# Graph attention on one core: picked keys enter VectorE's addition from PSUM with their factor moved into the exponential

## What is computed

```python
Q, K, V = ((nodes @ w + b).reshape(n, 8, 16) for w, b in (q, k, v))
row, col = edge_index                       # edges are sorted by col in the input; row groups the sums here
scores = (Q[row] * K[col]).sum(-1) / 4 + (Q[row] * (edge_attr @ we + be).reshape(-1, 8, 16)).sum(-1) / 4
es = exp(scores)                            # no maximum is taken off
w = es / (segment_sum(es, row)[row] + 1e-8)
out = segment_sum(w[..., None] * V[col], row).reshape(n, 128) @ wo + bo
```

## Time and profile before

| | |
|---|---|
| median of three runs | 4229.77 us |
| profiled execution, its own time | 4231.56 us |
| span of the profile | 4229.8 us |
| mean granted clock of TensorE | 0.958 |
| attention loop, 101 quads | 2407 to 4150 us |

### The profile page before, as it was taken

How to read it: one execution, slowest core, us unless ns; L and a number is a source line. 1 busy time by engine, 2 the same in 40 slices (tenths; PEclk the granted TensorE clock), 3 DMA queues, 4 the chain that set the end, 5 groups by cost and what they waited for, 6 DMA issues and landing times.

```text
span 4229.8 us, 87319 instructions
## 1 busy us (share of the span) xinstructions
PE 3654.2 (86%) x23947; PEld 2567.9 (61%) x23948; DVE 2605.3 (62%) x5758; ACT 1613.4 (38%) x4192; POOL 2980.4 (70%) x2979
## 2 busy tenths in 40 slices
PE   5557777259999999999997799999999999999993
PEld 3234444134454544544544488888888888888883
DVE  8999999131131221311313588888888888888887
ACT  0046666130010100100101466666666666666661
POOL 3148788777777777777777477777777777777770
PEclk8979999679999999999998899999999999999997
DMA  9635465469999999899997366666666666666661
GB/s 371 236 106 197 184 223 186 143 227 356 340 312 357 314 333 357 296 358 330 329 357 237 119 177 178 179 178 179 177 177 177 180 179 178 176 179 178 179 179 46
DMA packets 496864, 969.13 MB, mean 229 GB/s; under 512 B 279879, under 2 KB 297235, under 8 KB 494888
## 3 DMA queue, kind: packets, MB, share of 16 engines
q1 hardware_dynamic: 346872, 630.29, 44.8%
q0 software_dynamic: 118768, 243.12, 19.3%
q10 hardware_dynamic: 31168, 95.09, 6.8%
HBM read 767.81 MB, written 200.41 MB: 229 GB/s over the span
## 4 chain that ended last, share of the span: by engine, by line
PE 44%; POOL 31%; issue 13%; DVE 3%; DMA 2%; ACT 1%; DVEq 0%; POOLq 0%; ACTq 0%; SPq 0%
POOL records L1037 26%; PE ps L1158 12%; PE ps L1816 7%; PE ps L1834 7%; PE ps L1820 6%; POOL kv L1755 5%; PE ps L1809 3%; PE ps L1826 2%; PE ps L1789 2%; PE ps L1787 2%; PE ps L1444 1%; DMA records<-recs,pos 1%; PE ps L1136 1%; DMA kv<-kv_table,rec 1%; PE ps L1798 1%
## 5 line engine op out<-in xcount | busy, mean ns | idle before, releaser
L1037 POOL DMA_INDIRECT records<-recs,pos x1562 | 1586.7, 1016 | 480.7 <-issue 470.3
L1755 POOL DMA_INDIRECT kv<-kv_table,rec x1314 | 1311.2, 998 | 481.3 <-issue 440.7
L1158 PE MATMUL ps<-adj,mh 128*128 128x500 f16 (+1 forms) x6370 | 1308.3, 366 | 7.0 <-DVE mh L1309 6.1
L1158 PEld LDWEIGHTS ps<-adj,mh 128*128 128x128 f16 x6370 | 619.4, 97 | 674.8 <-DVE mh L1309 6.3
L1330 DVE TENSOR_TENSOR adj<-adj,quarter 128x128 f16<-128x128 f16 (+25 forms) x305 | 45.8, 209 | 764.7 <-DMA adj<-adj_full 756.8
L1820 PE MATMUL ps<-we,at 128*128 128x256 f32 x1616 | 466.3, 381 | 0.0
L1196 ACT ACTIVATE sc<-sc 128x1 f32<-128x1 f32 x6 | 1.2, 203 | 1216.1 <-DVE sc L1278 973.1
L1834 PE MATMUL ps<-msg,ohf 128*128 128x136 f32 x3232 | 449.0, 282 | 7.8 <-DVE msg L2006 7.8
L1816 PE MATMUL ps<-qn,oht 128*128 x3232 | 446.1, 281 | 4.2 <-ACT at L1883 1.2
L1816 PEld LDWEIGHTS ps<-qn,oht 128*128 128x128 f32 x3232 | 392.7, 192 | 47.4 <-issue 46.7
L1834 PEld LDWEIGHTS ps<-msg,ohf 128*128 128x128 f32 x3232 | 404.9, 191 | 8.9 <-DVE h L2024 8.8
(11 more groups left out here) (328 smaller groups left out, 5075.0 us busy)
## 6 DMA issues: line engine op xcount, KB each, us to landing
adj<-adj_full SPq DMA_DIRECT2D x420, 875.0 KB, 6.2
x1t<-kv_table SPq DMA_DIRECT2D x303, 256.0 KB
adj_full<-blk SPq DMA_DIRECT2D x12, 6125.0 KB, 19.0
records<-deg ACTq DMA_DIRECT2D x1, 56576.0 KB, 170.4
rec<-records SPq DMA_DIRECT2D x404, 136.0 KB
records<-recs,pos POOLq DMA_INDIRECT x1562
recs<-in_edge_attr ACTq DMA_DIRECT2D x18, 1344.0 KB, 13.3
kv<-kv_table,rec POOLq DMA_INDIRECT x1314
```

The costliest lines, as they stand in the source:

```text
L1037: G.indirect_dma_start(out=k.rec_d, out_offset=bass.IndirectOffsetOnAxis(ap=k.pos[:, at:at + 1], axis=0), in_=k.recs[:, q, j, :], in_offse ...
L1158: last = mm(bank, mh[:, part, hi, :], adj[:, c, x * width:(x + 1) * width], start=(hi == 0 and part == 0), stop=True, skip_group_check=True)
L1755: G.indirect_dma_start(out=kv[:, q, j, :], out_offset=None, in_=k.kv_d, in_offset=bass.IndirectOffsetOnAxis(ap=rec[:, q, j, RD:RD + 1].bit ...
```

## The change

The key lift goes from ScalarE's list. VectorE's addition takes all four tiles in every group; in a picked group the first tile of `kv` holds zero in its key half, written once before the loop, since no gather writes that slot, and so key and edge feature come from PSUM alone. What `goodcol` did for the keys is done in the exponential: for the first tile of a picked group the scale is a new column `goodscale` = 1/4 x `goodcol` (a marked group then gets exp(0) = 1, which its zeroed one-hot takes out of the sums). So the exponential of a picked group becomes two activations, one over tiles 1 to 3 and one over tile 0. `lifted` counts the values alone.

```diff
-            act.sem_inc(lifted, 2 * NPICK)
+            act.sem_inc(lifted, NPICK)
...
-            def lift_keys(g, q, i):
-                if q not in PICKS:
-                    return
-                done(act, "queried", g)
-                before(act, "scored", g, S)
-                act.sem_inc(sem("rec_gated"), 1)
-                A.activation(kq[:, q % S, 0, :], PS[:, 4 + q % S, 0:D], ACT.Identity, scale=goodcol[:, bass.ds(g, 1)]).then_inc(lifted, 1)
...
-                A.activation(msg[:, q, :, D:MW], sc[:, q % S, :].rearrange("p (j h) -> p j h", h=HEADS), ACT.Exp,
-                             scale=DK ** -0.5).then_inc(S_["weighed"], 1)
-            steps(act, ENG.Activation, ((lift_keys, 2), (pack, 0), (evacuate, 1), (weigh, 2), (lift_values, 2)))
+                j = GT - gathered(q)
+                scores = sc[:, q % S, :].rearrange("p (j h) -> p j h", h=HEADS)
+                last = A.activation(msg[:, q, j:GT, D:MW], scores[:, j:GT, :], ACT.Exp, scale=DK ** -0.5)
+                if j:
+                    last = A.activation(msg[:, q, 0, D:MW], scores[:, 0, :], ACT.Exp, scale=goodscale[:, bass.ds(g, 1)])
+                last.then_inc(S_["weighed"], 1)
+            steps(act, ENG.Activation, ((pack, 0), (evacuate, 1), (weigh, 2), (lift_values, 2)))
...
+            for q in PICKS:
+                V.memset(kv[:, q, 0, 0:D], 0.0)
             v.wait_ge(ends_spread, 1)
+            V.tensor_scalar(goodscale, PS[:, 1, 0:NG], DK ** -0.5, None, ALU.mult)
...
-                j = GT - gathered(q)
-                if j:
-                    v.wait_ge(lifted, i * (2 * NPICK) + (2 * (PICKS.index(q) + NPICK) + 1))
-                ch.link(V.tensor_tensor(kq[:, q % S, j:GT, :], kv[:, q, j:GT, 0:D], PS[:, 4 + q % S, j * P:].rearrange("p (j c) -> p j c", c=D), ALU.add))
+                ch.link(V.tensor_tensor(kq[:, q % S, :, :], kv[:, q, :, 0:D], PS[:, 4 + q % S, :].rearrange("p (j c) -> p j c", c=D), ALU.add))
```

More of the change, by code:

```diff
@@ L1603, in attend @@
         basecol = of(k.x1t, NG).bitcast(I32)
-        goodcol, badcol = of(k.x1t, NG), of(k.x1t, NG)
+        goodcol, badcol, goodscale = of(k.x1t, NG), of(k.x1t, NG), of(k.x1t, NG)
         given[0] = 0
@@ L1621, in attend @@
         wl = [sem(f"rows_loaded{q}") for q in range(len(PICKS))]
-        spotted, picked, lifted = sem("spots_turned"), sem("values_picked"), sem("keys_and_values_lifted")
+        spotted, picked, lifted = sem("spots_turned"), sem("values_picked"), sem("picked_values_lifted")
         NPICK, NONE = len(PICKS), 65536.0
@@ L2011, in message @@
                 if q in PICKS:
-                    v.wait_ge(lifted, i * (2 * NPICK) + (2 * (PICKS.index(q) + NPICK) + 2))
+                    v.wait_ge(lifted, i * NPICK + (PICKS.index(q) + 1 + NPICK))
                 weighted(q, slice(0, GT)).then_inc(S_["messages"], 1)
```

## The result

Six runs of the changed kernel took 4202.67 to 4210.26 us, median **4205.09**; six of the kernel before, beside them, 4226.74 to 4234.28, median 4229.32. The ratio is 0.9944 with a 95% interval of 0.9931 to 0.9957: 24 us faster, where 50 and a median of 4180 were forecast. The profiled execution took 4209.28 us (span 4207.5, mean granted clock 0.956) against 4231.56.

The account below looks back on a forecast made before the run. TensorE sets the pace with a ring through ScalarE's key lift over it. Quad 17.10 to 16.60 us (larger of 16.54 and 16.57, plus 0.03 jitter) gains 50 us, less 0.5 for the table: 4180 us, own range 4168 to 4196.

Parts of the forecast that it names:

- Restarts of TensorE: Attention loop, query product L1816: two late starts of 0.28 us a quad go, 0.56 us in all.
- VectorE's wait for the lift: Before VectorE's first addition: the 90.2 us wait goes, 1.02 us a quad; the key matmul is late next.
- VectorE's own quad: VectorE in the loop: 16.36 us a quad with wider additions (0.40 us), under TensorE's 16.54, so covered.
- Second exponential, tables: ScalarE's added exponential: 0.2 us each, cost nothing; extra column table and memsets ahead of the loop: 0.5 us.
- Gap at the loop's turn: TensorE's 0.54 us gap before the value pick L1809, once a quad, was left in unchanged.
- case D: Rival: the gap where the loop turns shrinks too and gathers hold 16.45 us; 4164 us, chance 0.06.
- Gathers: GpSimd's queue is late next: 16.45 us plus 0.12 for late starts gives 16.57 a quad, just over TensorE's 16.54.
- The quick quad: GpSimd at the slack end: needs 16.45 us with 12.46 busy, against 17.10 with 13.11 in a usual quad.
- The stretch of the gathers: GpSimd's 13 gathers: 0.76 us of stretch in the usual quad, 0.11 in the quick one used for the pace.
- Case A: Rival: GpSimd takes the pace with half its 0.76 us stretch left, 16.84 us a quad; 4204 us, chance 0.20.
- Case C: Rival: gathers lose step with VectorE and fall on its blockers at random, 17.43 us a quad; 4263 us, chance 0.06.

Follow-up runs that it names:

- j2: Kernel before with ScalarE's key lift moved behind the pack, nothing left out: 4214.14 us, ratio 0.9961.
- f5: Changed kernel with twelve gathers a quad and the addition only 384 wide in picked groups (tile 0's key and edge feature left out): 4150.56 us, ratio 0.9816.
- f1: Changed kernel with twelve gathers a quad instead of 13 (fourth group's first tile zero, not gathered): 4176.65 us, ratio 0.9877.
- f2: Kernel before with twelve gathers a quad instead of 13 (fourth group's first tile left out): 4225.06 us, ratio 0.9988.
- f3: Changed kernel with VectorE's message product moved ahead of its score in each turn, nothing left out: 4231.25 us, ratio 1.0005.

## Why the prediction was half right

- **Restarts of TensorE.** Right: no wait at L1816, all eight-matmul pieces 0.89 us, 2 x 0.28 us a quad gone. j2 shows their cause.
- **VectorE's wait for the lift.** Right: gone, and the key matmul late in its place (17.6 us). The addition takes 682 ns in all groups.
- **VectorE's own quad, 16.36 us, under TensorE's 16.54.** Wrong in both sizes, by amounts that hid each other. f5 ran at 16.35 and so TensorE can do with less than 16.54; and since taking 0.40 us from VectorE moved the quad, VectorE, which also idles 0.84 us at the loop's turn, helps to hold the changed loop at 16.60. I had put the wider addition's cost at nothing; it was 0.25 us a quad. That the ordinary quad came out at the forecast 16.60 is luck: the forecast had it from GpSimd's 16.57 and 0.03 for jitter, and f1 shows that GpSimd does not set it.
- **Second exponential, tables.** Right: nothing, though 287 ns and not 200.
- **Gap at the loop's turn.** "I leave it in": it fell to 0.22 us, as in case D, and the restart of 0.26 us at L1834 took that back.
- **Gathers: the step that failed.** "once in eight quads a gather starts 0.99 us late", "0.12 us a quad", "GpSimd's own pace is thus 16.45 + 0.12 = 16.57", and then "the larger of 16.54 and 16.57". The stall was spread over eight quads as if the four groups that GpSimd works ahead could even it out. They can't here: with 13 gathers GpSimd is 12.64 us busy and idles 13 x 0.30, which makes 16.54 of an ordinary quad's 16.60, and of what it loses it wins next to nothing back, so that each stall makes a quad longer than the pace that others set. The term should have been added, not compared. It measured 14.7 us for eleven stalls, 1.34 each (2.1 to 2.2 us of idle in ten of the twelve, where I took 1.29 from one row; in the kernel before itself five of twelve were 1.9 or more), and 4.05 us for the twelfth with its slow landing and its lower clock; and 13.4 us for the gathers that land late, which the sum did not have at all. f1 removed 32.0 us by giving the queue 1.16 us of margin, with all else in place. (The profiled execution lies 4.2 us above its runs' median, so the sizes are rather at the upper end.) The 4.7 us ahead of the first turn made up for a little.
- **The quick quad.** "In the quads at the slack end it needs 16.45 us" was read as what the queue can do at any time. Of the kernel before, the fast quads of the queue are those in which it catches up: that one is two quads behind the late gather of 3789.93. Its usual quad looked as full as now, 13.11 + 13 x 0.30 = 17.01 of 17.10 us, but held 0.76 us of stretch that it could shed, and the addition of a fourth group came 3.8 us after its last issue, where it now comes 3.2 us after it. The change took from both covers.
- **The stretch of the gathers.** I had 0.11 us left of 0.76 a quad; 0.33 stayed (12.64 - 13 x 0.947). Case A took half. Its time, 4204, is the measured one, but its mechanism is not: A has every quad at 16.84, and here 76 of 100 ran at a mean of 16.60.
- **Case C** did not come; the gathers that VectorE's message product catches are few enough (with the one-hot they stretch an ordinary quad's 13 by the 0.33 us above).

In the Trainium skill, "SBUF — State Buffer", section "Who interferes with whom", a VectorE instruction with two SBUF inputs contends with a GpSimd instruction that reads SBUF, and one with at most one such input does not. The trace agrees with both halves: the gather at 2619.51 starts inside the addition of 2619.20, which has one input in PSUM, and takes 0.95 us; the one at 2622.01 starts inside the message product of 2621.89, which has two in SBUF, and takes 1.40. Over the loop of the kernel before, from 2450 to 4100 us, the 590 gathers that start inside the addition, the query product or the sum per head took at most 0.96 us, and the 218 that start inside the message product a median of 1.22 and up to 1.46.

**Open.** What makes GpSimd idle once in 104 gathers (105 with twelve a quad). f1 and f2 show that it goes by the count of gathers and not by the quads or by time, no more. Also open is why this idle time is 0.7 us in one kernel and 1.29, 2.21 or 2.54 in others, and why certain gathers land late in every run; other contents of the table were not tried. And no kernel here that computes everything beat the changed one.

## What to carry to other kernels

An engine or queue that is within 1% of the pace is not hidden: look not at its mean but at what pays for its stalls. That can be time in which it waits for its consumer (here the 1.16 us in f1), stretch in its own instructions that it sheds when late, or a wait of the consumer for something else (both in the kernel before, where it idled no more than after). Rare delays are added to the steady pace when there is no such margin, and compared with it when there is. When an operation is removed, try first whether moving it gives the same: one line of order gave three quarters of this gain.

## What the runs showed of the hardware

An indirect gather of 128 rows costs GpSimd 0.947 us and 0.30 us between two. At every 104th or 105th gather comes an idle stretch, of 1.28 to 2.55 us in the kernel before, 0.95 to 2.21 in the changed one and 0.70 to 1.32 in f3. Landing follows the issue by 1.9 us in the median and by up to 4.2 us in the changed kernel and 3.6 us before (5.2 for the loop's last group), for largely the same groups. TensorE's granted clock was 0.50 from 2971 to 2974 us of the changed kernel, after it had idled 1.22 and 1.04 us. An exponential of 128x8 with its factor from a column takes 287 ns, one of 128x24 with a constant factor 223.
